# Block 0 of a four-block graph network: part of the value gathers moved beside counts and scores, messages left in one fp32 piece

## The reference

```
src = randint(0, 625);  dst = sort(int(625 * uniform ** 2))          # 10000 edges
h = layer_norm(x); q, k, v = split(h @ Wqkv + bqkv)                  # 8 heads of 64
logits = sum(q[src] * k[dst])                # per edge and head, q scaled by 512 ** -0.5
a = logits + dist_attn + path_attn
e = exp(a - segment_max(a, dst));  s = segment_sum(e, dst)
msg = v[src] * (e / s[dst])
agg = segment_sum(msg, dst)                  # 625 x 512
x = agg @ Wo + bo;  h1 = node_feature + x;  ...MLP, norm...
```

## Time and profile before

| | |
|---|---|
| median of 3 runs | 1493.08 us (1492.35 to 1493.74) |
| profiled execution | 1493.92 us, its span 1492.1 us |
| busy: PE, DVE, ACT, POOL | 1149.3, 915.8, 522.6, 301.2 us |
| edge stage | 205.07 to 484.2 us from the span's start |
| after it | 1007.9 us |

### The profile page before, as it was taken

The page is one execution under the profiler, slowest core; times in us unless marked ns, Lnnn a source line. Parts: engine busy times, 40 slices in busy tenths (PEclk is TensorE's granted clock), DMA queues, the critical chain, the costliest instruction groups (busy, mean ns, idle before and its releaser), DMA issues.

```text
span 1492.1 us, 15704 instructions
## 1 busy us (share of the span) xinstructions
PE 1149.3 (77%) x5598; PEld 899.6 (60%) x5599; DVE 915.8 (61%) x1620; ACT 522.6 (35%) x774; POOL 301.2 (20%) x358
## 2 busy tenths in 40 slices
PE   6987913333435799979988999999988998785884
PEld 4545512222324698769867986788777977533552
DVE  5686645546455735566766576566666665576895
ACT  1201942222122344224522452344432351023781
POOL 1050037777774100010000000000000000112001
PEclk9978955555555899979999999999999999897997
DMA  6050633232230422122101120102010210200001
GB/s 192 0 145 1 223 115 84 65 76 71 70 81 4 156 79 65 56 98 72 43 29 57 39 76 8 50 29 92 23 57 29 88 47 22 62 1 0 1 1 35
DMA packets 47060, 90.98 MB, mean 61 GB/s; under 512 B 17138, under 2 KB 17538, under 8 KB 45721
## 3 DMA queue, kind: packets, MB, share of 16 engines
q1 hardware_dynamic: 26516, 69.12, 14.2%
q0 software_dynamic: 20480, 20.99, 5.8%
HBM read 72.01 MB, written 17.91 MB: 60 GB/s over the span
## 4 chain that ended last, share of the span: by engine, by line
PE 53%; DVE 18%; POOL 11%; issue 8%; ACT 5%; DMA 3%; SPq 1%; DVEq 0%; POOLq 0%; ACTq 0%
PE ps L1500 13%; PE ps L1447 10%; PE ps L1475 9%; POOL arena L536 5%; POOL logit_ring L536 5%; PE ps L1480 4%; PE ps L1637 4%; PE ps L1534 3%; PE ps L1463 3%; DMA logits_scratch<-arena 2%; DVE arena L1402 2%; DVE arena L1401 2%; ACT arena L635 2%; PE ps L1583 1%; DVE arena L1167 1%
## 5 line engine op out<-in xcount | busy, mean ns | idle before, releaser
L1608 PE MATMUL ps<-messages_r,onehot_r 125*125 125x512 f32 x192 | 97.5, 659 | 187.8 <-issue 120.0
L1447 PE MATMUL ps<-arena 125*128 125x314 f32 (+3 forms) x768 | 216.3, 438 | 8.1 <-DVE arena L977 4.1
L522 POOL TENSOR_TENSOR var_eps<-mean_var,ln_consts 125x1 f32<-125x1 f32 x70 | 17.6, 251 | 869.6 <-DVE mean_var L1153 583.5
L1447 PEld LDWEIGHTS ps<-arena 125*128 125x128 f32 (+3 forms) x768 | 136.4, 182 | 78.1 <-DVE neg_max L987 8.4
L1608 PEld LDWEIGHTS ps<-messages_r,onehot_r 125*125 125x125 f32 x192 | 47.5, 306 | 197.8 <-issue 190.8
L1534 PE MATMUL ps<-ident,arena 125*125 125x125 f32 x625 | 80.3, 282 | 27.7 <-ACT arena L822 15.8
L536 POOL DMA_INDIRECT arena<-value_scratch,idx_ring x64 | 94.6, 1479 | 29.2 <-issue 14.6
L1534 PEld LDWEIGHTS ps<-ident,arena 125*125 125x125 f32 x625 | 75.0, 193 | 35.6 <-ACT arena L822 17.8
L536 POOL DMA_INDIRECT logit_ring<-logits_scratch,idx_ring x64 | 82.9, 1296 | 20.2 <-issue 19.2
L1002 DVE TENSOR_TENSOR edge_logits<-logit_ring,arena 125x32 f32<-125x32 f32 x20 | 3.8, 192 | 126.7 <-DMA logit_ring<-logits_scratch,idx_ring 104.5
L1475 PE MATMUL ps<-input_high,weight_high 128*128 128x314 f32 x320 | 72.9, 309 | 1.6 <-DVE weight_low L1137 1.6
(11 more groups left out here) (256 smaller groups left out, 2853.5 us busy)
## 6 DMA issues: line engine op xcount, KB each, us to landing
logits_scratch<-arena SPq DMA_DIRECT2D x5, 2187.5 KB
arena<-in_m_w SPq DMA_DIRECT2D x8, 1024.0 KB, 6.4
arena<-in_w_up SPq DMA_DIRECT2D x4, 1024.0 KB, 5.3
arena<-in_w_down SPq DMA_DIRECT2D x4, 1024.0 KB, 7.6
arena<-in_wq SPq DMA_DIRECT2D x4, 1024.0 KB, 5.4
arena<-in_wk SPq DMA_DIRECT2D x4, 1024.0 KB, 5.3
arena<-in_wv SPq DMA_DIRECT2D x4, 1024.0 KB, 5.4
arena<-in_wo SPq DMA_DIRECT2D x4, 1024.0 KB, 5.5
```

The lines of the kernel that those rows point to most:

```text
L1447: last = mm(out_view[:, place:place + HALF_W], w, r[:, lo:lo + HALF_W], start=n == 0, stop=n == len(pairs) - 1)
L1608: mm(ps[0:TILE, 512 * j:512 * j + 512], onehot, MSGR[:, HALF * hf + u, part, :], start=False, stop=True, skip_group_check=True)
```

## The change

- Front: the indices are loaded ahead of x; the values are projected before queries and keys; the first one-hots are made while x is on its way.
- Counts: the one-hot ring holds seven groups instead of four; ACT, not DVE, copies the counts to SBUF, and DVE makes the mask tile by tile.
- Gathers of values: a ring of 14 slots of four chunks in place of four. The gathers of groups 0 to 8 (36 of 80) are issued ahead of the edge stage, group 0 once the values are stored, groups 1 to 8 once the conditioning parts are done (their slots lie over its buffers and over the projections' weights). Inside, each of the first 11 groups issues its logits and the values of the group nine later; the last nine only logits.
- The index ring and its copies go; gathers take their index from `src_i` and `pair_i` directly, in a loop that is written out.
- Messages and probabilities stay in fp32: no high and low parts, one fp32 product for each chunk and tile. ACT makes only Exp there. The loops of counts and edges are written out on PE, DVE, ACT and POOL.
- The first slots lie over x, so x is loaded again in the edge stage, and Wo after the staging buffers are stored. The split of Wo in high and low moves to groups 16 and 17 of the edge stage.

The diff, cut:

```diff
+        OHF = at(R_Q, 2, HALF, W, p=TILE)
+        PROBS = at(R_O, 4, HALF * H0, p=TILE)
-        VG = [at(R_P + HALF * D * r, HALF, D, p=TILE) for r in range(3)] + [at(R_Y, HALF, D, p=TILE)]
+        EARLY_V = 9
+        SLOTS = ([R_X + HALF * D * n for n in range(3)] + [R_P + HALF * D * n for n in range(6)]
+                 + [R_W + HALF * D * n for n in (0, 1, 2, 3, 5)])
+        VG = [at(offset, HALF, D, p=TILE) for offset in SLOTS]
+
+        def slot_of(group):
+            return group if group < len(SLOTS) else group - len(SLOTS) + 3
...
-        A = ring("front", [("t", k) for k in range(FT)]
+        A = ring("front", [("t", k) for k in range(FT)] + [("v", n) for n in range(3)]
...
+            load(dst_i[:, :], dst_t, "idx")
+            load(src_i[:, :], src_t, "idx")
             node_transfer(X, rows_view(x), "ld_x")
...
+            sp.wait_ge(sig("msg_group_free"), 3)
+            load(WO0, feat_view(w_o0), "wo0")
+            node_transfer(X, rows_view(x), "ld_x")
             sp.wait_ge(sig("agg_done"), 1)
...
+            gather_values(0)
+            A.wait_filled(pool, ("cond",))
+            for key in (("hid",), ("cond",)):
+                A.wait_evacuated(pool, key)
+            pool.wait_ge(sig("cond_parts_ready0"), 1)
+            for group in range(1, EARLY_V):
+                gather_values(group)
             pool.wait_ge(sig("pairs_ready"), 1)
             for j in range(2):
                 pool.wait_ge(sig(f"stage_stored{j}"), 32 * ((NT + 1 - j) // 2))
...
+            for group in range(GROUPS):
+                if group >= 4:
+                    pool.wait_ge(sig("edge_logits_ready"), group - 3)
+                gather_logits(group)
+                ahead = group + EARLY_V
+                if ahead < GROUPS:
+                    if ahead >= len(SLOTS):
+                        pool.wait_ge(sig("msg_group_free"), slot_of(ahead) + 1)
+                    gather_values(ahead)
...
+            act.wait_ge(sig("counts_done"), 1)
+            for j in range(NT):
+                a.activation(C2[:, j, 0:512], ps[0:TILE, 512 * j:512 * j + 512], ACT.Copy)
+                a.activation(C2[:, j, 512:W], ps[0:TILE, 2560 + 128 * j:2560 + 128 * j + W - 512], ACT.Copy
+                             ).then_inc(sig("counts_ready"), 1)
...
+            for group in range(GROUPS):
+                act.wait_ge(sig("edge_logits_ready"), group + 1)
+                if group >= 4:
+                    act.wait_ge(sig("msg_group_free"), group - 3)
+                a.activation(PROBS[:, group % 4, :], sum_ring[:, group % 2, :], ACT.Exp).then_inc(sig("edge_probs_ready"), 1)
+                if group == GROUPS - 4:
+                    one_weight_high("wo0", WO0, 2)
...
+            for group in range(GROUPS):
+                hf, slot = group % 2, slot_of(group)
+                if group >= 2:
+                    dve.wait_ge(sig("msg_group_free"), group - 1)
+                for u in range(HALF):
+                    v.tensor_scalar(OHF[:, hf, u, :], iota16[0:TILE, :], dst_f[:, HALF * group + u:HALF * group + u + 1], None,
+                                    ALU.is_equal)
...
+                dve.wait_ge(sig("edge_probs_ready"), group + 1)
+                dve.wait_ge(sig(landing(group)[0]), landing(group)[1])
+                for u in range(HALF):
+                    last = v.tensor_tensor(VG[slot][:, u, :].rearrange("p (h d) -> p h d", h=H0),
...
+                last.then_inc(sig("msg_ready"), 1)
+                if group == GROUPS - 3:
+                    one_weight_low(1, WO0, 2)
...
-                                for part in range(2):
-                                    mm(ps[0:TILE, 512 * j:512 * j + 512], onehot, MSGR[:, HALF * hf + u, part, :],
-                                       start=False, stop=True, skip_group_check=True)
...
+                            mm(ps[0:TILE, 512 * j:512 * j + 512], onehot, VG[slot][:, u, :], start=False, stop=True, skip_group_check=True)
+                            mm(ps[0:TILE, 2560 + H0 * j:2560 + H0 * (j + 1)], onehot, PROBS[:, group % 4, u * H0:(u + 1) * H0],
+                               start=False, stop=True, skip_group_check=True)
```

More of the change, by code:

```diff
@@ L196, in build, with landing @@
+        VG = [at(offset, HALF, D, p=TILE) for offset in SLOTS]
+        def slot_of(group):
+            return group if group < len(SLOTS) else group - len(SLOTS) + 3
+        LATE = 5
+        def landing(group):
+            if group < EARLY_V:
+                return "values_early", 16 * HALF * EARLY_V
+            turn, k = divmod(group - EARLY_V, LATE)
+            return f"values_late{k}", 16 * HALF * (turn + 1)
         HT0 = at(R_V, FF0, W)
@@ L407, in _ @@
             load(ATTR[:, 1, :], attr_b, "attr")
-            load(WO0, feat_view(w_o0), "wo0")
             load(cw1[:, :, :], feat_view(c_w1), "c")
@@ L532, in _, with gather_values, gather_logits @@
             g.partition_all_reduce(gflag[:, 1, :], gflag[:, 0, :], TILE, bass.bass_isa.ReduceOp.max).then_inc(sig("flags_all"), 1)
-            def gather(dst, table, name, index):
+            def gather_values(group):
+                slot, landed = slot_of(group), landing(group)
+                if group >= EARLY_V + LATE:
+                    pool.wait_ge(sig(landed[0]), landed[1] - 16 * HALF)
                 for u in range(HALF):
-                    g.indirect_dma_start(dst(u), None, table, bass.IndirectOffsetOnAxis(ap=index(u), axis=0)
-                                         ).then_inc(sig(name), 16)
-            def gather_values(half, index):
-                gather(lambda u: VG[half % 4][:, u, :], v0_d, f"values_gathered{half % 4}", index)
-            def gather_logits(half, index):
-                gather(lambda u: lg_ring[:, half % 4, u * H0:(u + 1) * H0], logits_d, f"logits_gathered{half % 4}", index)
+                    c = HALF * group + u
+                    g.indirect_dma_start(VG[slot][:, u, :], None, v0_d, bass.IndirectOffsetOnAxis(ap=src_i[:, c:c + 1], axis=0)
+                                         ).then_inc(sig(landed[0]), 16)
+            def gather_logits(group):
+                for u in range(HALF):
+                    c = HALF * group + u
+                    g.indirect_dma_start(lg_ring[:, group % 4, u * H0:(u + 1) * H0], None, logits_d,
+                                         bass.IndirectOffsetOnAxis(ap=pair_i[:, c:c + 1], axis=0)
+                                         ).then_inc(sig(f"logits_gathered{group % 4}"), 16)
             pool.wait_ge(sig("v0_stored"), 32)
             pool.wait_ge(sig("ld_idx"), 32)
-            for half in range(4):
-                gather_values(half, lambda u: src_i[:, HALF * half + u:HALF * half + u + 1])
+            gather_values(0)
[5 more added lines that the diff above has]
+                gather_values(group)
             pool.wait_ge(sig("pairs_ready"), 1)
@@ L864, in _, with onehot_group @@
             v.memset(NOISE[:, NODES:W], 0.0)
+            dve.wait_ge(sig("ld_idx"), 32)
+            v.tensor_copy(src_f[:, :], src_i[:, :])
+            dve_chain(dve, v.tensor_copy(dst_f[:, :], dst_i[:, :]))
+            def onehot_group(group):
+                if group >= AHEAD:
+                    dve.wait_ge(sig("onehot_group_free"), group - AHEAD + 1)
+                for u in range(HALF):
+                    slot, c = group % AHEAD * HALF + u, HALF * group + u
+                    v.tensor_scalar(OH16[:, 0, slot, :], iota16[0:TILE, :], dst_f[:, c:c + 1], None, ALU.is_equal)
+                    last = v.tensor_scalar(OH16[:, 1, slot, :], iota16[0:TILE, :], src_f[:, c:c + 1], None, ALU.is_equal)
+                last.then_inc(sig("onehot_ready"), 1)
+            dve.wait_ge(sig("iota_ready"), 1)
+            onehot_group(0)
             dve.wait_ge(sig("ld_x"), 32)
@@ L891, in _, with bank_view, row_bias @@
             v.tensor_scalar(TURNS, PHASE, 3.1415925, -3.1415925, ALU.min, ALU.max).then_inc(sig("emb_ready"), 1)
+            def bank_view(r, key, pair):
+                return r.view(key).rearrange("p (b c) -> p b c", b=2)[:, 0:len(pair), :]
+            def row_bias(r, key, pair, dst, row):
+                r.wait_filled(dve, key)
+                r.release(key, v.tensor_tensor(dst[:, pair[0]:pair[-1] + 1, :], bank_view(r, key, pair),
+                                               row.to_broadcast([TILE, len(pair), D]), ALU.add))
+            onehot_group(1)
+            dve.wait_ge(sig("ld_rows0"), 16)
+            for n, pair in enumerate(PAIRS):
+                row_bias(A, ("v", n), pair, V, ROWS[:, 0:1, :])
+                if n == 0:
+                    onehot_group(2)
             def queries0(k):
@@ L896, in queries0 @@
                                                     col("bq", k), float(D) ** -0.5, ALU.add, ALU.mult))
-            def onehot_pair(slot, c):
-                v.tensor_scalar(OH16[:, 0, slot, :], iota16[0:TILE, :], dst_f[:, c], None, ALU.is_equal)
```

(5 more changed lines are left out.)

217 lines of the change are left out of this document (64 added, 153 removed).

## The result

The changed kernel took 1433.29 us, the median of 4 runs (1429.56 to 1436.68), the kernel before, measured together with it, 1493.41 (1492.35 to 1497.05): a ratio of 0.959, 95% interval 0.956 to 0.963, some 60 us or 4% faster. The forecast was 1443, ten more; the time lies in its range.

A forecast was written before the change was run, and what follows sets the result against it. POOL's indirect gathers were taken to bound the edge stage. POOL's -55.8, the tail's +4.0, the front's +1.6 and -0.3 sum to -50.5 us on the profiled 1493.92: 1443.4, stated as 1443, range 1426 to 1468.

The forecast's parts named there:

- (a): Edge stage on POOL: 20 value gathers fewer (64 to 44) at 1.78 us each, 35.6 us less.
- (b): Edge stage on POOL: without index ring, 16 copy gaps of 0.93 us, one copy and a slot wait go: 17.5 less.
- (c): Edge stage: less DVE work beside POOL's gathers slows them less, in proportion to that work; 2.7 us expected.
- (d): Counts: 32 value gathers moved ahead run from near 82 to 130 us, hidden, at no cost.
- (e): Edge stage's end: unsplit fp32 products put PE behind POOL in the last groups; tail 21.5 us against 17.5, plus 4.0.
- The rival of a tail at half clock: Last edge groups: PE runs at half clock, total 1487, half-way 1465; chance 0.14 of landing above 1458.
- (f): Tail: DVE's 5.3 us a group stays under PE's 5.9; the wo0 split, 2.3 us on DVE, is hidden.
- (g): Front through scores: index loads ahead of x plus 1.1 us, counts copied by ACT plus 0.5; together plus 1.6.
- the second rival: Counts get shorter, and the tail may run at full clock with POOL unslowed: 15 us less, 1428; chance 0.15.
- (h): Later loads of x and wo0 cost nothing; one reduction less ahead of the norm: -0.3 us.
- The rival of skipped code: Counts and tail: PE's jumps over unneeded written-out tile blocks cost up to 0.6 us more each, total 1508; chance 0.07.

The follow-up runs named there:

- the load back: The changed kernel with four extra DVE subtractions a group behind the messages, into room nobody reads: 1447.62 us, ratio 0.970.
- the quarter product: The changed kernel with PE multiplying only 128 of the 512 message columns from group 11 on: 1426.83 us, ratio 0.956.
- the run with the last tile first: The changed kernel with value gathers spread over 18 turns, and PE testing receiver tiles from the last down from group 10 on: 1423.00 us, ratio 0.954.

## Why the prediction held, step by step

**What bounds the kernel** was read rightly: the edge stage is POOL's, and 55.4 of the ledger's 63.4 us are there.

**(a), 20 gathers fewer.** Right in kind, 29.5 us in place of 35.6. The term took a gather's mean over the stage, 1.78 us with its gap. The gathers that stay are slower on average once those leave (logit gathers 1.28 us with four groups early, 1.33 with nine): DVE has the same 20 groups to make and disturbs as many gathers, 40 or 44, so a gather taken out is worth its undisturbed 1.51, not the mean.

**(b), the index ring.** 17.5 expected; the written-out loop with copies gives 18.6, the copies 1.9, 20.5 together. Of the 20.5, 15.2 are gaps, near the 14.9 of the 16 turns in the term, and the rest shorter gathers that it didn't have. The size was near, the cause as the prediction put it ("0.93 us lost by the copies") was two thirds wrong: 0.31 a turn are the copies, 0.61 went with the loop. A gap was put down to the instructions that stand in it.

**(c), less DVE beside the gathers.** 2.7 expected. The two sides of it, from 241.1 without copies to 235.7 with all of the change but the gathers, are 5.4 us: 3.0 of shorter gathers, and 2.6 of a wait for DVE in the first turn. The prediction was right that DVE is what slows a gather: in the edge stages of these kernels no gather with DVE idle beside it takes over 1.22 us. Its rule for the size, slowing in proportion to DVE's work, fell: with the load back the gathers took the same 168.6 us in sum. Which DVE instruction costs a gather 0.3 us, 0.5 or nothing is open. And 3.0 us are no more than the gathers' sum moves between kernels with one edge stage (168.8, 167.3 and 164.4), so (c) is not shown apart from that spread.

That (a), (b) and (c) sum to 55.8 and POOL's part shrank by 55.4 is then partly luck: -6.1, +3.0 and +2.7 cancel.

**(d), hidden in the counts.** Held: 32 gathers run from 82.40 us on, at a mean of 1.21 us, and the last ends at 130.57, half a microsecond behind the counts, with nobody waiting. (Group 0's four began at 59.10, not near 49; nothing waits for them either.) They do slow DVE's one-hots: with the gathers behind the counts a pair takes 0.38 + 0.38 us, with them 0.54 + 0.37 on average, or 0.58 and 0.76 from start to start; once in each gather one of the one-hots takes 0.72. With seven groups ahead this stays under PE, whose counts last 50.0 us either way. The Trainium skill (SBUF — State Buffer, SBUF: two separate sides) has a DMA issued from GpSimd pay beside a DVE copy, 620 ns becoming 3100. In the counts the trace does not agree: the gathers keep their 1.21 us and DVE pays, 0.18 us a pair. In the edge stage it agrees in kind: gathers beside DVE take up to some 1.7 us, and one 3.27. What the prediction didn't ask is why the counts and not the scores: there the same gathers cost some 12 us.

**(e), the tail.** +4.0 expected, +2.1 measured. The chunk at full clock is 1.08 us for the forecast's 1.16, 0.08 on 48 chunks being 3.8. The forecast had PE behind POOL from group 12 on, with 1.0 us of gap a group as in the earlier trace rows. The trace has it otherwise: where a group's messages lie ready, it follows with no gap (410.29), but three times PE runs empty (375.96, 398.28 and 417.81), for 2.05, 2.55 and 2.89 us, and each time two or three of the next chunks run at or near half clock. The wait for messages is only 0.39, 0.45 and 0.27 of it; the rest, 1.65, 2.10 and 2.61, is the start behind two, three and four failed tests, which a group pays when its messages come later than PE. At the last the lateness is to be seen: DVE could begin the one-hots only when PE had ended the group two before (410.39). So the forecast had the sum nearly right and the course wrong. That PE's products, not POOL, set this end is shown by the quarter product. A third buffer of one-hots was not tried. The rival of a tail at half clock came only in those few chunks: the granted clock is 0.82 and 0.91 in the last two stretches.

**(f)** The forecast had DVE's 5.3 us a group under PE's 5.9. Measured, DVE takes 4.81 from one-hots to messages (410.39 to 415.20) and PE 4.64 for a group of one tile (410.29 to 414.93): the margin is not there, and the two buffers tie one to the other. The low part of wo0 took DVE 2.3 us at 396; it shows in no wait, but the logit gather beside it took 3.27 us, 2.06 more than undisturbed, which the forecast did not have.

**(g), the front.** +0.5 for +1.1, and the copies on ACT take 3.4 us, not 4.6: ten of 3.35 us in all. The counts were put at no change and were 4.8 shorter; this is the step that failed. The term looked at PE's gaps (9.5 us before, 9.8 after, the same), and took seven groups ahead for a convenience: with a ring of four and the 32 gathers beside it DVE is busy for 49 of 55 us and done 4 us before PE, and the ring of seven takes 12 pairs, 9 us of DVE, out of it. (In the kernel before, with 16 gathers, DVE was done at 127.3, 7 us ahead of PE, and the counts took as long; what held PE back there was not separated.) It is the first half of the second rival, by another route than its gaps. The granted clock in the counts rose too, from 0.75 to 0.90 (0.85 with the ring of four), and PE's 512-column products fell from 503 to 441 ns.

**(h), all that follows.** -3.4 for -0.3. In the runs above 1004.2 to 1010.2 us are seen from the reciprocal on, where their code is the same; so this is taken for a spread between executions.

**The rival of skipped code** was right that failed tests cost time: from messages to first product it takes 1.0 us with none (the run with the last tile first), then 1.27, 1.65, 2.10 and 2.61 with one to four (groups 11, 14, 17 and 19 of the changed kernel), some 0.4 a skip, and wrong on the sum: only groups that PE waits for pay it; where messages lie ready, the skips show in no gap. The looped kernel before shows nearly the same, 2.5 us. Code fetched from memory rises (instruction queue q8 61 packets, 43 before) with no wait that can be tied to it.

## What to carry to other kernels

A gap between two instructions is not the cost of what stands in it: take the small instructions out and keep the loop, then the other way round, before one is blamed. Work moved to an idle engine is hidden only if the DMA engines have room as well: 32 gathers were free in the counts (DMA share 0.58 with them) and cost some 12 us beside the stores of the logits (0.87). And where two stages are unevenly loaded by the same stream of gathers, spreading them can be worth as much (10 us here) as an edit that makes the stream shorter.

## What the runs showed of the hardware

- A loop on POOL with register offsets and a semaphore increment, as it stood here, costs 0.61 us a turn in the gap ahead of an indirect gather (0.91 to 0.30); 144 gathers of the same kind took 200.6 us in it and 192.2 and 195.3 written out.
- A bf16 one-hot of 628 columns on DVE takes 0.38 us alone; beside indirect gathers one in four takes 0.72, and the gathers keep 1.21 us.
- In the edge stage a gather with DVE idle beside it takes 1.21 to 1.22 us; all 44 of 124 over 1.25 us have a DVE instruction beside them, one of 3.27 us a subtraction of 2.28. Four subtractions more a group left their sum as it was (168.6 against 168.8 us).
- PE's first product behind four skipped blocks comes 2.6 us after what it waited for, with three 2.1, with two 1.65, with one 1.27, with none 1.0; where the work lay ready no gap shows (410.29).
- An fp32 product of 512 columns with one of 8 columns behind it takes 1.08 us at full clock and 2.13 near half (417.81 on: 419.49 to 421.62).
- Behind a gap of 2.9 us in PE the first two products run near half clock, where products of groups that follow without one are at full clock.
